# Attention block in one launch: the second normalised tensor's high part, the fourth inner cast and the last transposition change their places

## The chip, the cores and the metric

The kernel runs on one core of one Trainium2 chip. The core has TensorE for matrix products and transpositions (in the profile PE, its weight loads PEld), VectorE (DVE), ScalarE (ACT) and GpSimd (POOL) for elementwise work, and SyncE (SP), which here does nothing but start DMAs. The metric is the device time of one execution in microseconds. The kernel before takes 1758.4 us, the median of three runs from 1757.55 to 1760.98.

## The reference

The inputs are x and memory of 128 sequences by 128 rows by 256 features, a mask, and the weights of one block with 16 heads of 16 features:

```
tgt1 = layer_norm(x, g1, be1)
q, k, v = tgt1 @ Wq.T + bq, tgt1 @ Wk.T + bk, tgt1 @ Wv.T + bv
p = softmax(q k.T / 4 + (1 - mask) * -1e9)         # 16 heads
t = x + (p v) @ Wo.T + bo + (memory @ Wg.T + bg)
z = layer_norm(t, g2, be2)
out = t + relu(z @ W1.T + b1) @ W2.T + b2           # 256 -> 1024 -> 256
```

All of it is in fp32. The large products are made of three passes each: both operands are split into a high part (the value rounded to the type fp32r) and a low part (the rest), and a product is high by low, low by high, high by high. So each operand of a product costs a copy (the high part) and a subtraction (the low part), on whatever engine they are placed.

## The kernel before, in words

The 128 sequences are worked off in 64 groups of two. A loop over `i` from -2 to 65 is written out in full, and each pass works on several groups at once, one stage each: `norm` (first layer norm of group i+2), `front` (q, k and v of group i+1), `attn_` (scores, exponentials, transpositions of group i), `out_` (values, output product and second layer norm of group i-1) and `ffn` (the inner layer of group i-2). Each engine has its own copy of the loop, and within a pass 13 ticks `t`; what an engine does in what order is written out by hand as `if stage and t == n`, in program order. Engines wait for each other by semaphores alone, and an engine that waits holds up all that stands behind it on its queue. A pass takes some 26.4 us.

The second layer norm runs like this. TensorE makes the output product (ticks 5 and 6). VectorE adds the residual and takes the statistics (tick 7), GpSimd makes the inverse root (`rstd`, L867 and L869), VectorE makes the normalised tensor `xhat` in two instructions, one for each sequence (tick 8, `layer_norm_apply`, L617), and turns it in blocks of 32 by 32 into the buffer `attn` (`turn_quads`, L626). Four DMAs from SP bring the blocks back into `xhat` with the features on the partitions (L392). ScalarE then makes z's high part (`zT_hi`, `split_high`, L441, tick 12), VectorE its low part (`zT_lo`, L733, tick 0 of the next pass), and TensorE starts the first of four inner products with it (`up`, tick 1). ScalarE applies the relu to each of the four (ticks 3, 4, 5 and 7, L501), VectorE makes the high part (`hidden_high`, a CAST, L684), GpSimd the low part (`split_low`, L874), and TensorE contracts each of the four pairs back (`DOWN_TICKS`, 9 to 12).

On ScalarE the `zT_hi` of tick 12 stands ahead of `copy_inverses` (L468, the transposed inverse sums), and both ahead of the next pass's `copy_turned` of the last chunk (L460) and the first chunk's exponentials (L448). Later in that pass come `q_hi` (L488), further exponentials, the first relu (L501) and `k_hi` (L515), for which VectorE's `k_lo` (L788) waits. On VectorE the fourth `hidden_high` stands behind `xhat` and its transposition (L811 and L812), ahead of `v_pad`, `mask_bias` and the reciprocals. On GpSimd the fourth `hT_lo` stands behind `rstd` and ahead of `xT_hi` and `xT_lo` (L918, L923), the split of the first layer norm's tensor for the group behind.

Of the kernel before, what the change touches and what calls it, by code (L numbers as in the profile page):

```python
# [58 lines left out]
def is_at(i, n):  # L59

    return isinstance(i, int) and i == n
# [7 lines left out]
def xattn_block(nc, x, memory, mask, wqT, wkT, wvT, woT, wgT, w1T, w2T,  # L69
# [26 lines left out]
    with ExitStack() as ctx:  # L96
# [70 lines left out]
        for name, n in VECTORS:  # L167
# [56 lines left out]
        proj_ready, xres_biased, resid_ready = sem("proj_ready"), sem("xres_biased"), sem("resid_ready")  # L224
        ln2_stats, ln2_mean, ln2_var, ln2_rstd, ln2_ready = (
            sem(f"ln2_{n}") for n in ("stats", "mean", "var", "rstd", "ready"))
        z_blocked, z_cols, z_hi, z_split = (sem(f"z_{n}") for n in ("blocked", "cols", "hi", "split"))

        hid_ready, hid_relu, hid_hi, hid_split = (sem(f"s_hid_{n}") for n in ("ready", "relu", "hi", "split"))
# [92 lines left out]
        def _(sp):  # L322
# [29 lines left out]
            def iteration(i, norm, front, attn_, out_, ffn):  # L352
                if front:

                    g = i + 1
                    if g < 2:
                        sp.wait_ge(zeros_set, 2 * g + 2)
                    else:
                        sp.wait_ge(scores_ready, CHUNKS * (g - 1))
                    sp.wait_ge(q_split, g + 1)  # L360
                    for j, high_low in enumerate((1, 0, 0)):
                        sp.dma_start(q_stack[g % 2][j:P:CPB].bitcast(F32),
                                     q[high_low][:].bitcast(F32)).then_inc(q_stacked, 16)
                    sp.wait_ge(k_split, g + 1)
                    for e in range(2):
                        for j, high_low in enumerate((0, 1, 0)):
                            to = HALF * e + j
                            sp.dma_start(k_stack[g % 2][to:HALF * (e + 1):CPB, :, e].bitcast(F32),
                                         kk[high_low][HALF * e:HALF * (e + 1)].bitcast(F32)
                                         ).then_inc(k_stacked, 16)  # L370
                    if known(i, 1, GROUPS):
                        sp.wait_ge(mem_split, i)
                        sp.dma_start(mem_in[:], mem_cols[i]).then_inc(mem_loaded, 16)
                if is_at(i, GROUPS - 1):

                    sp.wait_ge(mem_split, i)
                    sp.dma_start(mem_in[:], mem_cols[i]).then_inc(mem_loaded, 16)
                if norm and i + 2 > 0:

                    sp.wait_ge(x_blocked, i + 2)  # L380
                    for n in range(QUADS):
                        sp.dma_start(x_flat[:, n * P:(n + 1) * P],
                                     x_blocks[32 * n:32 * (n + 1), :].rearrange("c (j n) -> c j n", j=QUADS)
                                     ).then_inc(x_cols, 16)
                if known(i, 1, GROUPS):
                    sp.wait_ge(resid_ready, i)
                    sp.dma_start(x_res[:], x_rows[i]).then_inc(xres_loaded, 16)
                if out_:

                    sp.wait_ge(z_blocked, i)  # L390
                    for n in range(QUADS):
                        sp.dma_start(xhat2_flat[:, n * P:(n + 1) * P],  # L392
                                     attn_blocks[32 * n:32 * (n + 1), :].rearrange("c (j n) -> c j n", j=QUADS)
                                     ).then_inc(z_cols, 16)
                if known(i, -1, GROUPS - 2):
                    sp.wait_ge(bias_ready, i + 2)
                    sp.dma_start(mask_in[:], mask_rows[i + 2]).then_inc(mask_loaded, 16)
                if known(i, -2, GROUPS - 3):
                    if i == -2:
                        sp.wait_ge(ln1_ready, 1)  # L400
                    elif i == -1:
                        sp.wait_ge(x_split, 2)
                    else:
                        sp.wait_ge(x_pool_split, i + 1)
                    sp.dma_start(x_in[:], x_rows[i + 3]).then_inc(x_loaded, 16)
                if attn_:

                    sp.wait_ge(inv_copied, i + 1)
                    if later(i):
                        sp.wait_ge(attn_ready, i)  # L410
                    heads = P // SPREADS
                    for b in range(GB):
                        for k in range(KT):
                            at = heads * (KT * b + k)
                            sp.dma_start(inv[:, k, b * S:(b + 1) * S],
                                         inv_cols[at:at + heads, :].unsqueeze(1)
                                         .broadcast_to([heads, P // heads, S])).then_inc(inv_spread, 16)
                if ffn:

                    sp.wait_ge(y_summed, i - 1)  # L420
                    sp.dma_start(out_rows[i - 2], y[:]).then_inc(y_stored, 16)
# [5 lines left out]
        def _(act):  # L427
# [42 lines left out]
            def iteration(i, norm, front, attn_, out_, ffn):  # L470
                for t in range(TICKS):
                    if out_ and t == 0:
                        copy_turned(i - 1, CHUNKS - 1)
                    if is_at(i, -1) and t == 0:
                        split_high(by_tile[1], xT[0][:], x_turned, 1, v_ready, None, x_hi)
                    if attn_ and t == EXP_TICKS[0]:
# [40 lines left out]
                        last.then_inc(k_high, 1)  # L517
                    if attn_ and t in (4, 6, 7, 9):
                        exponentials(i, CPB + (4, 6, 7, 9).index(t))
                    if out_ and t == 12:  # L520
                        g = i - 1
                        split_high(quad_cols(xhat2), in_order(zT[0]), z_cols, 16 * QUADS * (g + 1), hid_ready,
                                   HJ * g if later(g) else None, z_hi)
                    if attn_ and t == 12:
                        copy_inverses(i)

# [16 lines left out]
        def _(dve):  # L543
# [147 lines left out]
            def iteration(i, norm, front, attn_, out_, ffn):  # L691
                for t in range(TICKS):
# [18 lines left out]
                    if attn_ and t < CHUNKS:  # L711
# [15 lines left out]
                                in1=mask_bias[:, b, :], scale=1.0, scalar=HIGHEST, op0=ALU.add,  # L727
                                op1=ALU.min, accum_out=row_min[:, t, h:h + 1])
                        last.then_inc(scores_masked, 1)
                    if ffn and t == 0:  # L730
                        g = i - 2
                        dve.wait_ge(z_hi, g + 1)
                        dve.tensor_tensor(in_order(zT[1]), quad_cols(xhat2), in_order(zT[0]), ALU.subtract  # L733
                                          ).then_inc(z_split, 1)
# [37 lines left out]
                        dve.tensor_copy(attnT[0][:], attn[:]).then_inc(attnT_hi, 1)  # L772
                    if out_ and t == 4:
                        split_low(attn[:], attnT, attnT_hi, i, attnT_split)
                    if ffn and t in HIDDEN_TICKS and t < 8:
                        hidden_high(i - 2, HIDDEN_TICKS.index(t))
                    if norm and t == 4 and i != -1:
                        dve.wait_ge(x_loaded, 16 * (i + 3))
# [25 lines left out]
                    if out_ and t == 8:  # L804
                        g = i - 1
                        if later(g):
                            dve.wait_ge(z_split, g)
                        layer_norm_apply(g, resid, mv2, rstd2, ln2_rstd, xhat2, ln2_ready)
                        dve.wait_ge(attnT_split, g + 1)
                        turn_quads(attn_blocks, xhat2, ln2_ready, g + 1, z_blocked)  # L810
                    if ffn and t == HIDDEN_TICKS[-1]:  # L811
                        hidden_high(i - 2, HJ - 1)  # L812
                    if front and t == 9:
                        set_values(i + 1, 0)
                        set_values(i + 1, 1)
# [20 lines left out]
        def _(pool):  # L836
# [39 lines left out]
            def iteration(i, norm, front, attn_, out_, ffn):  # L876
                for t in range(TICKS):
                    if norm and t == 5:
                        inverse_root(i + 2, mv1, var1, rstd1, ln1_mean, ln1_var, ln1_ready, ln1_rstd)
                    if ffn and t in HIDDEN_TICKS:  # L880
                        g, n = i - 2, HIDDEN_TICKS.index(t)
                        if n == 0 and later(g):
                            pool.wait_ge(down_ready, g)
                        split_low(hid[:, n % 2], [h[:, 2 * n:2 * n + 2, :] for h in hT], hid_hi,
                                  HJ * g + n + 1, hid_split)
                    if out_ and t == 2:
                        g = i - 1
                        pool.wait_ge(mem_loaded, 16 * (g + 1))
# [40 lines left out]
        def _(pe):  # L929
# [122 lines left out]
            def iteration(i, norm, front, attn_, out_, ffn):  # L1052
                fronts, outs = stages_before(i)
                for t in range(TICKS):
# [60 lines left out]
                        last.then_inc(v_ready, 1)  # L1115
                    if ffn and t in UP_TICKS:
                        up(i, t)
                    if ffn and t in DOWN_TICKS:

                        g, part = i - 2, DOWN_TICKS.index(t)  # L1120
                        if part == 0 and i < GROUPS:
                            pe.wait_ge(hid_relu, HJ * g + HJ)
                        elif part == 0:
                            pe.wait_ge(y_summed, g)
                        pe.wait_ge(hid_split, HJ * g + part + 1)
                        for f in range(2 * part, 2 * part + 2):
                            for b in range(GB):
                                last = product(ffn_ps[:, b * D:(b + 1) * D],
                                               [(cut(hT, ALL, f, seq(b)), cut(w2, ALL, f))],
                                               start=(f == 0 and b == 0), stop=(f == FT - 1),  # L1130
                                               skip_group_check=True)
                        if part == HJ - 1:
                            last.then_inc(down_ready, 1)
# [44 lines left out]
```

## Time and profile before

| what | value |
|---|---|
| median of the runs | 1758.4 us |
| the profiled execution | 1759.22 us |
| its span, first to last instruction | 1757.3 us |
| PE busy | 1684.2 us, 96% |
| PEld busy | 1643.0 us, 93% |
| DVE busy | 1509.3 us, 86% |
| ACT busy | 1393.1 us, 79% |
| POOL busy | 953.5 us, 54% |
| granted TensorE clock, mean | 0.99 of full speed |

The busy shares are means over the whole span. The profile's 40 slices show the same pattern from the third to the last but one: the 64 groups are worked off in passes that are almost alike. What sets the length of a pass is read from the timeline of one pass; the passes between about 849 and 876 us are used below. In a timeline row the first number is the start in microseconds from the span's start, the second the time the row takes (for xN all of them), and the brackets say how long the engine was idle before and for whom it waited.

### The profile page before, as it was taken

Reading aid. Unit: us, or ns where it says so; the run is one execution under the profiler, and the core shown is the slowest. Engines: PE = TensorE matmul, PEld = TensorE weight load, DVE = VectorE, ACT = ScalarE, POOL = GpSimd, SP = SyncE. Lnnn points to the kernel's source line nnn. Section 1 sums busy time; section 2 is a strip of 40 time slices with the busy share of each in tenths; the row PEclk is TensorE's granted clock in tenths of the full one; section 3 lists DMA queues with packets and bytes.
Section 4 is the critical chain, followed back from the end, with each engine's and each line's share of the span. In section 5 each row is a group of like instructions: output and inputs, shape, how many; then the busy total and the mean of one; then the engine's idle time right before and its main releaser. Section 6 shows DMA issues by size and latency. Waiting matters only on the chain. (4 is left out here: it accounts for less than half of the span.)

```text
span 1757.3 us, 53486 instructions
## 1 busy us (share of the span) xinstructions
PE 1684.2 (96%) x17272; PEld 1643.0 (93%) x17272; DVE 1509.3 (86%) x7136; ACT 1393.1 (79%) x5506; POOL 953.5 (54%) x906
## 2 busy tenths in 40 slices
PE   6799999999999999999999999999999999999997
PEld 5699999999999999999999999999999999999997
DVE  7798898898888888888888888888888888888873
ACT  4788788788788788788788788788788787787782
POOL 5355545545545545555555555555555555555544
PEclk8899999999999999999999999999999999999999
DMA  5434444444444444444444444444444444444421
GB/s 187 130 124 138 140 131 138 131 139 132 134 142 130 137 140 130 136 141 131 136 145 128 136 142 131 135 142 132 134 139 136 133 141 135 128 146 135 128 91 37
DMA packets 258951, 233.77 MB, mean 133 GB/s; under 512 B 26992, under 2 KB 209136, under 8 KB 258672
## 3 DMA queue, kind: packets, MB, share of 16 engines
q1 hardware_dynamic: 258672, 230.35, 41.5%
q8 instruction: 139, 2.28, 0.6%
q14 instruction: 140, 1.15, 0.2%
HBM read 62.73 MB, written 16.78 MB: 45 GB/s over the span
## 5 line engine op out<-in xcount | busy, mean ns | idle before, releaser
L448 ACT ACTIVATE scores<-scores,row_min 128x128 f32<-128x128 f32 x2048 | 799.5, 406 | 37.1 <-DVE row_min L725 37.1
L874 POOL TENSOR_TENSOR hT_lo<-hid,hT_hi 128x512 fp32r<-128x512 f32 x256 | 339.6, 1327 | 687.7 <-DVE hT_hi L684 687.7
L725 DVE CUSTOM_DVE_ANT_0 scores<-score_ps,mask_bias 128x128 f32<-128x128 f32 x2048 | 467.8, 286 | 1.5 <-issue 1.1
L448 ACT ACTIVATION_READ_ACCUMULATOR scores<-scores,row_min 128x1 f32 x2048 | 420.5, 205 | 0.0
L460 ACT ACTIVATE probs<-turn_ps 128x512 f32<-128x512 f32 x512 | 306.3, 599 | 92.6 <-PE turn_ps L1022 92.6
L956 PE MATMUL ffn_ps<-w_hi,hT_lo 128*128 128x256 f32 x1024 | 301.2, 294 | 32.6 <-POOL hT_lo L874 32.2
L1022 PE MATMUL turn_ps<-ident,scores 128*128 128x128 f32 x2048 | 307.1, 273 | 5.3 <-ACT probs L460 5.3
L956 PE MATMUL ffn_ps<-zT_hi,w_lo 128*128 128x256 f32 x992 | 294.0, 296 | 1.4 <-ACT hid L501 1.2
L958 PE MATMUL ffn_ps<-w_hi,hT_hi 128*128 128x256 f32 x1024 | 284.2, 277 | 0.0
L957 PE MATMUL ffn_ps<-w_lo,hT_hi 128*128 128x256 f32 x1024 | 283.5, 277 | 0.0
L957 PE MATMUL ffn_ps<-zT_lo,w_hi 128*128 128x256 f32 x992 | 276.1, 278 | 0.0
L958 PE MATMUL ffn_ps<-zT_hi,w_hi 128*128 128x256 f32 x992 | 275.5, 278 | 0.0
L501 ACT ACTIVATE hid<-ffn_ps,vec 128x256 f32<-128x256 f32 x496 | 208.6, 481 | 43.9 <-PE ffn_ps L958 43.8
L1022 PEld LDWEIGHTS turn_ps<-ident,scores 128*128 128x128 f32 x2048 | 235.2, 140 | 6.1 <-ACT scores L448 6.1
L956 PEld LDWEIGHTS ffn_ps<-w_hi,hT_lo 128*128 128x128 f32 x1024 | 192.4, 188 | 47.3 <-POOL hT_lo L874 46.6
L1008 PE MATMUL score_ps<-k_stack,q_stack 128*128 128x256 f32 x1024 | 206.7, 294 | 2.3 <-DVE row_min L725 2.3
L956 PEld LDWEIGHTS ffn_ps<-zT_hi,w_lo 128*128 128x128 f32 x992 | 187.2, 189 | 14.6 <-issue 12.3
L957 PEld LDWEIGHTS ffn_ps<-w_lo,hT_hi 128*128 128x128 f32 x1024 | 193.0, 189 | 0.0
L958 PEld LDWEIGHTS ffn_ps<-w_hi,hT_hi 128*128 128x128 f32 x1024 | 192.3, 188 | 0.0
L957 PEld LDWEIGHTS ffn_ps<-zT_lo,w_hi 128*128 128x128 f32 x992 | 187.0, 188 | 0.0
L958 PEld LDWEIGHTS ffn_ps<-zT_hi,w_hi 128*128 128x128 f32 x992 | 186.3, 188 | 0.0
L725 DVE DVE_READ_ACCUMULATOR2_ANT row_min<- 128x1 f32 x2048 | 168.9, 82 | 0.0
(144 smaller groups left out, 4288.0 us busy)
## 6 DMA issues: line engine op xcount, KB each, us to landing
q_stack<-q_hi SPq DMA_DIRECT2D x128, 256.0 KB, 2.4
k_stack<-k_hi SPq DMA_DIRECT2D x256, 128.0 KB, 2.3
x_in<-x_dram SPq DMA_DIRECT2D x64, 256.0 KB, 2.7
mem_in<-memory_dram SPq DMA_DIRECT2D x64, 256.0 KB, 3.0
x_res<-x_dram SPq DMA_DIRECT2D x64, 256.0 KB, 3.0
q_stack<-q_lo SPq DMA_DIRECT2D x64, 256.0 KB, 2.3
k_stack<-k_lo SPq DMA_DIRECT2D x128, 128.0 KB, 2.3
inv<-inv_cols SPq DMA_DIRECT2D x256, 64.0 KB, 2.4
```

What stands on the lines that cost most here:

```text
L448: last = act.activation(exps, exps, ACT.Exp, bias=row_min[:, k, h:h + 1], scale=-1.0, accum_out=row_sum[:, k, h:h + 1])
L460: act.activation(probs[:, k, :], turn_ps[k % 2][:, :], ACT.Copy).then_inc(probs_copied[k % 2], 1)
L501: last = act.activation(hid[:, n % 2, j, :], up_bank(i, n)[:, j * ROWS:(j + 1) * ROWS], ACT.Relu, bias=b1c[:, 2 * n + j:2 * n + j + 1])
L725: last = dve.tensor_tensor_reduce(out=scores[:, slot(i, t), h, :], in0=score_ps[t % 2][:, h * S:(h + 1) * S], in1=mask_bias[:, b, :], scal ...
L874: pool.tensor_tensor(halves[1], src, halves[0], ALU.subtract).then_inc(done, 1)
L956: pe.matmul(dst, lhs[1], rhs[0], start=start and j == 0, stop=False, **more)
L957: pe.matmul(dst, lhs[0], rhs[1], start=False, stop=False, **more)
L958: last = pe.matmul(dst, lhs[0], rhs[0], start=False, stop=stop and j == n - 1, **more)
L1008: last = pe.matmul(score_ps[n % 2][:, k * 2 * S:(k + 1) * 2 * S], q_stack[i % 2][:, c, k, seq(b)], k_stack[i % 2][:, c, :, GB * k + b, :], ...
L1022: last = pe.transpose(turn_ps[k % 2][:, h * S:(h + 1) * S], scores[:, slot(g, k), h, :], ident[:])
```

## The change

Four things are edited, and a semaphore `z_turned` is added.

1. On ScalarE, `zT_hi` leaves tick 12 and stands at tick 0 of the next pass, behind `copy_turned` of the last chunk and ahead of the first exponentials. `copy_inverses` and that `copy_turned` so come ahead of it.
2. On VectorE, `zT_lo` goes from tick 0 to tick 1, behind the masking of the second chunk's scores.
3. On VectorE, all four `hidden_high` are now issued in the same place of their ticks, so the fourth (tick 8) comes ahead of `xhat` and its transposition.
4. For the last group alone, `xhat` isn't turned in blocks and moved by the four DMAs. TensorE transposes it with four products by the identity into the bank `work[1]` (before the last contraction of pass 64), and ScalarE and VectorE take high and low part from there.

```diff
@@ SP, iteration
-                if out_:
+                if out_ and i < GROUPS:
 
                     sp.wait_ge(z_blocked, i)
@@ ScalarE, iteration
                     if out_ and t == 0:
                         copy_turned(i - 1, CHUNKS - 1)
+                    if is_at(i, GROUPS + 1) and t == 0:
+                        split_high(by_tile[1], zT[0][:], z_turned, 1, hid_ready, HJ * (GROUPS - 1), z_hi)
+                    elif ffn and t == 0:
+                        g = i - 2
+                        split_high(quad_cols(xhat2), in_order(zT[0]), z_cols, 16 * QUADS * (g + 1), hid_ready,
+                                   HJ * g if later(g) else None, z_hi)
...
-                    if out_ and t == 12:
-                        g = i - 1
-                        split_high(quad_cols(xhat2), in_order(zT[0]), z_cols, 16 * QUADS * (g + 1), hid_ready,
-                                   HJ * g if later(g) else None, z_hi)
                     if attn_ and t == 12:
                         copy_inverses(i)
@@ VectorE, iteration
-                    if ffn and t == 0:
+                    if is_at(i, GROUPS + 1) and t == 1:
+                        split_low(by_tile[1], zT, z_hi, GROUPS, z_split)
+                    elif ffn and t == 1:
                         g = i - 2
                         dve.wait_ge(z_hi, g + 1)
...
-                    if ffn and t in HIDDEN_TICKS and t < 8:
+                    if ffn and t in HIDDEN_TICKS:
                         hidden_high(i - 2, HIDDEN_TICKS.index(t))
...
                         layer_norm_apply(g, resid, mv2, rstd2, ln2_rstd, xhat2, ln2_ready)
-                        dve.wait_ge(attnT_split, g + 1)
-                        turn_quads(attn_blocks, xhat2, ln2_ready, g + 1, z_blocked)
-                    if ffn and t == HIDDEN_TICKS[-1]:
-                        hidden_high(i - 2, HJ - 1)
+                        if i < GROUPS:
+                            dve.wait_ge(attnT_split, g + 1)
+                            turn_quads(attn_blocks, xhat2, ln2_ready, g + 1, z_blocked)
@@ TensorE, iteration
+                    if is_at(i, GROUPS) and t == 12:
+                        pe.wait_ge(ln2_ready, GROUPS)
+                        pe.wait_ge(resid_ready, GROUPS)
+                        turn(by_tile[1], xhat2).then_inc(z_turned, 1)
                     if ffn and t in DOWN_TICKS:
```

VectorE's queue from the second layer norm's statistics to the addition that ends the inner layer, in a pass of the middle, before the change (the dots leave out the masking of one chunk's scores):

```order
L611 BN_AGGR mv<-stats 128x2 x2
...
L617 SCALAR_TENSOR_TENSOR xhat<-resid,mv,rstd 128x256 x2
L626 STREAM_TRANSPOSE attn<-xhat 128x2x4x32 x2
L684 CAST hT_hi<-hid 128x512
L666 TENSOR_TENSOR v_pad<-work_ps,row 128x8x16 x4
L821 TENSOR_SCALAR mask_bias<-mask_in 128x256
```

The same place of the same queue with the change:

```order
L614 BN_AGGR mv<-stats 128x2 x2
...
L687 CAST hT_hi<-hid 128x512
L620 SCALAR_TENSOR_TENSOR xhat<-resid,mv,rstd 128x256 x2
L629 STREAM_TRANSPOSE attn<-xhat 128x2x4x32 x2
L669 TENSOR_TENSOR v_pad<-work_ps,row 128x8x16 x4
L825 TENSOR_SCALAR mask_bias<-mask_in 128x256
```

The cast of the fourth inner pair has moved ahead of the two `xhat` instructions and the two transpositions; all else keeps its order.

ScalarE's queue across the boundary of two passes, before the change (`probs` are the turned chunks, `inv_cols` the inverse sums):

```order
L460 ACTIVATE probs<-turn_ps 128x512
L441 ACTIVATE zT_hi<-xhat 128x512
L468 ACTIVATE inv_cols<-turn_ps 128x128
L460 ACTIVATE probs<-turn_ps 128x512
L448 ACTIVATE scores,row_sum<-scores,row_min 128x128 x4
L488 ACTIVATE q_hi<-work_ps,qk_bias 128x256 x2
```

And with the change:

```order
L461 ACTIVATE probs<-turn_ps 128x512
L469 ACTIVATE inv_cols<-turn_ps 128x128
L461 ACTIVATE probs<-turn_ps 128x512
L442 ACTIVATE zT_hi<-xhat 128x512
L449 ACTIVATE scores,row_sum<-scores,row_min 128x128 x4
L495 ACTIVATE q_hi<-work_ps,qk_bias 128x256 x2
```

`zT_hi` has moved behind the inverse sums and the last turned chunk; it still stands ahead of the exponentials. GpSimd's queue is unchanged in order.

## Rows read from the trace of the kernel before

**Rows 1.** View of waits, whole span: who waited for whom, us, times, longest.

```profile
ACT zT_hi L441 <- DMA xhat<-attn: 148.6, 64, 7.0
...
PEld ffn_ps L956 <- POOL hT_lo L874: 46.6, 61, 1.4
...
PE ffn_ps L956 <- POOL hT_lo L874: 32.2, 61, 1.2
```

**Rows 2.** Timeline of TensorE at the fourth contraction of one pass.

```profile
871.81 0.60 PE L1022 MATMUL turn_ps<-ident,scores 128*128 128x128 f32 x4
872.90 0.38 PE L956 MATMUL ffn_ps<-w_hi,hT_lo 128*128 128x256 f32 x1 [0.49 <-POOL hT_lo L874]
```

**Rows 3.** Timeline of VectorE in the same pass.

```profile
859.41 0.84 DVE L788 SCALAR_TENSOR_TENSOR k_lo<-work_ps,qk_bias,k_hi 128x256 fp32r<-128x256 f32 x2
...
861.02 0.42 DVE L684 CAST hT_hi<-hid 128x512 fp32r<-128x512 f32 x1
861.36 1.92 DVE L617 SCALAR_TENSOR_TENSOR x_in<-x_in,mv,rstd 128x256 f32<-128x256 f32 x2
863.38 1.18 DVE L626 STREAM_TRANSPOSE x_quads<-x_in 128x256 f32<-128x256 f32 x2
...
868.48 0.28 DVE L725 CUSTOM_DVE_ANT_0 scores<-score_ps,mask_bias 128x128 f32<-128x128 f32 x1
869.03 0.88 DVE L617 SCALAR_TENSOR_TENSOR xhat<-resid,mv,rstd 128x256 f32<-128x256 f32 x2 [0.26 <-POOL rstd L869]
```

**Rows 4.** Timeline of GpSimd in the same pass.

```profile
861.52 1.47 POOL L874 TENSOR_TENSOR hT_lo<-hid,hT_hi 128x512 fp32r<-128x512 f32 x1 [0.67 <-DVE hT_hi L684]
...
868.24 0.69 POOL L869 TENSOR_TENSOR rstd<-var,minus_half 128x2 f32<-128x2 f32 x1
871.58 1.27 POOL L874 TENSOR_TENSOR hT_lo<-hid,hT_hi 128x512 fp32r<-128x512 f32 x1 [2.65 <-DVE hT_hi L684]
872.80 1.10 POOL L918 TENSOR_TENSOR xT_hi<-x_in,one 128x512 fp32r<-128x512 f32 x1
```

**Rows 5.** Timeline of ScalarE from one zT_hi to the next.

```profile
848.89 0.63 ACT L441 ACTIVATE zT_hi<-xhat 128x512 fp32r<-128x512 f32 x1 [2.21 <-DMA xhat<-attn]
849.43 0.26 ACT L468 ACTIVATE inv_cols<-turn_ps 128x128 f32<-128x128 f32 x1
...
850.07 0.40 ACT L448 ACTIVATE scores<-scores,row_min 128x128 f32<-128x128 f32 x1
...
855.40 0.84 ACT L501 ACTIVATE hid<-ffn_ps,vec 128x256 f32<-128x256 f32 x2
...
858.13 0.85 ACT L515 ACTIVATE k_hi<-work_ps,qk_bias 128x256 fp32r<-128x256 f32 x2
...
875.23 0.63 ACT L441 ACTIVATE zT_hi<-xhat 128x512 fp32r<-128x512 f32 x1 [2.18 <-DMA xhat<-attn]
```

**Rows 6.** Timeline of TensorE at the second inner product of that pass.

```profile
856.37 0.37 PE L956 MATMUL ffn_ps<-zT_hi,w_lo 128*128 128x256 f32 x1
```

**Rows 7.** Timelines of VectorE and GpSimd in the set-up.

```profile
21.80 1.00 POOL L869 TENSOR_TENSOR rstd<-var,minus_half 128x2 f32<-128x2 f32 x1
22.34 0.43 DVE L591 CAST wv_hi<-scores 128x512 fp32r<-128x512 f32 x1
26.28 4.98 POOL L856 TENSOR_TENSOR w_lo<-probs,w_hi 128x2048 fp32r<-128x2048 f32 x1
26.98 1.20 DVE L626 STREAM_TRANSPOSE x_quads<-x_in 128x256 f32<-128x256 f32 x2
```

**Rows 8.** The chain that ended last, its tail: start us, us, what.

```profile
1736.94 2.14 DMA xhat<-attn
...
1741.12 0.38 PE score_ps L956
```

**Rows 9.** View of stretches: busy us by engine, then the granted TensorE clock (1.00 is full).

```profile
1738.40:1741.10 2.70, 0.00 (x0) 0.00 (x0) 1.99 (x2) 0.63 (x1) 1.26 (x1) 1.00 0.34 114
1742.20:1745.60 3.40, 3.40 (x18) 3.40 (x18) 0.43 (x1) 0.84 (x2) 0.90 (x1) 0.51 0.00 0
```

More of the change, by code:

```diff
@@ L226, in xattn_block @@
             sem(f"ln2_{n}") for n in ("stats", "mean", "var", "rstd", "ready"))
+        z_turned = sem("z_turned")
         z_blocked, z_cols, z_hi, z_split = (sem(f"z_{n}") for n in ("blocked", "cols", "hi", "split"))
@@ L883, in iteration @@
                             pool.wait_ge(down_ready, g)
-                        split_low(hid[:, n % 2], [h[:, 2 * n:2 * n + 2, :] for h in hT], hid_hi,
-                                  HJ * g + n + 1, hid_split)
+                        split_low(hid[:, n % 2], [h[:, 2 * n:2 * n + 2, :] for h in hT],
+                                  hid_hi, HJ * g + n + 1, hid_split)
                     if out_ and t == 2:
```

## The prediction

> **What bounds the kernel now.** I read the page first, then the view of waits, then the timeline of one pass for each engine. The page shows TensorE busy nearly throughout, and 61 almost equal passes: the question is what sets the length of one. The view of waits [rows 1] gives TensorE one wait that comes in every pass: the low part of the inner layer from GpSimd, 46.6 us at its weight loads in 61 waits, 0.76 us each (32.2 us by the matmul rows, which count the end of the product before as busy; I take the larger, since TensorE starts its next product 1.09 us after the transposition of a chunk [rows 2] and nothing but the wait explains so long a step). The other wait of that size is ScalarE's for the DMAs of `xhat`, 148.6 us in 64, which holds TensorE up nowhere so far.
>
> The timeline says where the 0.76 us come from. The fourth cast of `hid` stands behind `xhat` and its transposition on VectorE, so GpSimd's subtraction runs from 871.58 to 872.85 [rows 4] and the fourth contraction begins at 872.90 [rows 2]. TensorE could have begun it at about 872.1.
>
> A pass is 26.34 us by the two `zT_hi` [rows 5]; over the 61 passes it is 26.4.
>
> **The change part by part.**
>
> The cast that moves ahead (edit 3). The masking of the eighth chunk ends at about 868.7 and `xhat` starts at 869.03 behind an idle time of 0.26 us for `rstd` [rows 3]. The cast takes the next instruction's place for 0.34 us (861.02 to 861.36, the same pair of rows [rows 3]), so it fits this idle time and `xhat` can still start at 869.03. GpSimd's subtraction starts 0.08 us after a cast ends (861.44 to 861.52 [rows 3, 4]), here at about 869.15 instead of 871.58, and is done near 870.5, where TensorE wants it at 872.1. The wait is gone: 0.76 us in each of 61 passes, 46.6 us. That is the whole gain if nothing else gives way.
>
> What gives way is `xhat`. The two instructions of `xhat` take 0.88 us, with GpSimd silent. The same operation on `x_in`, with the same shapes, takes 1.92 us [rows 3]: it stands directly behind the second cast, and GpSimd's subtraction starts 0.16 us after it and takes 1.47 us instead of 1.27 [rows 4]. So the two engines keep each other off: one half runs, then GpSimd's whole subtraction, then the other half. The change makes exactly this picture at `xhat`: cast, two such instructions, and a GpSimd subtraction that starts some 0.1 to 0.15 us after the first. The price is 1.92 - 0.88 = 1.04 us. From below it would be 0 (GpSimd as if silent), from above GpSimd's time before the first half and another GpSimd operation between the halves (a rival). I take 1.04, since it is the row nearest in every respect. The block transposition behind it pays nothing: in the set-up it took 1.20 us for its two in the middle of a GpSimd subtraction of 4.98 us, as 1.18 beside an idle GpSimd [rows 3, 7].
>
> [...]
>
> What hangs on `xhat`. It is followed by the transposition, the four DMAs and `zT_hi`: from the start of `xhat` to the start of `zT_hi` 875.23 - 869.03 = 6.20 us [rows 3, 5], now 7.24. Edit 1 takes the inverse sums and the chunk's copy out from behind `zT_hi`: from `zT_hi` to the exponentials it was 850.07 - 848.89 = 1.18 us and is now `zT_hi`'s own step, 849.43 - 848.89 = 0.54 [rows 5]. So ScalarE begins the exponentials 1.04 - 0.64 = 0.40 us later than before, where TensorE wants to be 0.76 earlier. It works without a gap from there: exponentials, `q_hi`, two more chunks, the first relu. That relu ends at 856.24 and TensorE's second inner product begins at 856.37 [rows 5, 6], with 0.13 us to spare. There TensorE will wait about 0.7 us; the wait has moved.
>
> Whether this is a loop of its own decides the length of a pass, so I close it. From the exponentials ScalarE needs 858.98 - 850.07 = 8.91 us to the end of `k_hi` [rows 5]; `k_lo` on VectorE waits for it (0.05 us for the hand-over); from `k_lo` VectorE works without a gap to `xhat`, 869.03 - 859.41 = 9.62 [rows 3]; then 6.20 to the next `zT_hi` and 0.54 to the exponentials. The sum is 8.91 + 0.05 + 9.62 + 6.20 + 0.54 = 25.32 us without the stall and 26.36 with it. TensorE alone would do with 26.34 - 0.76 = 25.58. The loop now is as long as the old pass of 26.34 to 26.40: the gain of 46.6 us is given back, but for 0 to 2 us; I take 1.
>
> In this loop DMAs that land late are paid in full, which ScalarE's idle time hid before. The wait for them is (148.6 - 7.0) / 63 = 2.25 us in the mean and 2.18 to 2.21 in the rows of a quiet pass [rows 1, 5]: 63 x 0.05 = 3 us if all is paid, 0 if none. I take 2.
>
> `zT_lo` one chunk later (edit 2). VectorE's second masking takes about 0.85 us and fills the time in which `zT_hi` isn't there. If GpSimd's next operation holds the subtraction up, it ends at about 878.3, and TensorE's first inner product starts at about 879: 0.6 us of cover, so nothing. If that cover were gone, it would cost what is missing, once a pass.
>
> GpSimd's `xT_hi` follows the fourth subtraction (872.80 [rows 4]) and comes 1.3 to 2.3 us earlier; nobody waited for it. SP's four DMAs keep their place; those behind them (mask, `x_in`, inverse rows) aren't held up by anything new.
>
> The last group (edit 4). Before, from the end of `xhat` to the first product: the transposition, the DMAs (the last of them 1736.94 to 1739.08), 0.6 us for the high part, 1.3 for the low part, product at 1741.12 [rows 8]. Now TensorE transposes behind its third contraction (about 0.5 us), and high and low part overlap the fourth contraction, the addition of `y` and 0.7 us of subtraction. I get the first product at about 1738.5, 2.6 us earlier. [...] So the tail gives 2.6 to 4.3 us; I take 4, with some tenths from `copy_inverses` coming earlier in pass 63.
>
> **The sum**, on the profiled execution: 1759.2 (span 1757.3 and 1.9 around it) - 1 + 2 - 4 = 1756.2. This execution is 0.8 above the median of the runs, so 1755.4 us.
>
> **The rivals.**
>
> *The stall stays out.* If `xhat` gets through beside GpSimd, the loop is 25.32 and TensorE binds with 25.58: ScalarE starts the exponentials 0.64 us earlier against TensorE's 0.76, and 0.13 of spare time covers the difference. Then 1759.2 - 46.6 + 2 - 4 - 0.8 = 1710 us. For it: the cause is read from another place. Against: the row of `x_in` has the same neighbours, and 61 such passes show it. Partial forms, a stall that eats half of the gain, lie near 1733. Together 0.22.
>
> *GpSimd gets in first.* The cast falls into GpSimd's `rstd` (868.24 to 868.93 [rows 4]). In the set-up an `rstd` with a VectorE cast over its end took 1.00 us instead of 0.69 and ended at 22.80, just behind the cast (22.77) [rows 7]. If that happens here, `rstd` ends near 869.08 and `xhat` starts near 869.18, with GpSimd's subtraction already begun. Then both halves wait for its end near 870.42: 0.15 + 1.24 + 0.88 instead of 1.92, 0.35 us more a pass, 61 x 0.35 = 21 us: 1776 us. If `xT_hi`, which is then ready, also goes between the halves (1.10 us [rows 4]), it is 1.45 us a pass, 88 us: 1844. The point from which it decides is the order of two starts, GpSimd's subtraction and the first `xhat`, which I see within 0.05 us of each other in this case. Against it: one row of the set-up carries it, and there other VectorE work also lay beside `rstd`. 0.14 for the mild form, 0.08 for the full one.
>
> **How the numbers follow.** My forecast, the wait that moves from GpSimd's subtraction to the relu, has 0.50 and by its own bounds lies between 1749 and 1762. The other two have 0.22 and 0.22, and 0.06 is left for what I don't see, evenly to both sides. What a measurement of this kernel can tell from no change is 0.2%, 3.5 us, so the line to faster is at 1754.9, in the middle of my forecast: 0.23 of its 0.50 is faster, 0.25 the same, 0.02 slower. With the rivals: faster 0.23 + 0.22 + 0.03 = 0.48, slower 0.02 + 0.22 + 0.03 = 0.27, the same 0.25. The range from 1706 to 1778 takes in the forecast, the first rival and the mild form of the second, 0.86, and leaves out its full form.
>
> **What would show it.** TensorE's wait for `hT_lo` falls from 46.6 us to a few. `xhat` takes 1.92 us for its two (0.88 refutes me towards 1710), starting before GpSimd's subtraction; if the subtraction comes first, the second rival holds. TensorE or its weight loads get a wait of 30 to 45 us in all for the relu of ScalarE (L508) at the second inner product, and `k_lo` follows `k_hi` at once. ScalarE's wait for the DMAs shrinks to some 0.3 to 0.8 us a pass, since it now does the inverse sums and a chunk's copy while they are under way. The passes stay at 26.3 to 26.4 us; at 25.6 my loop is wrong. In the tail the first product of the last group comes about 2.6 us earlier against the end of the third contraction, and the granted clock stays at 1.00 behind it or not.

## The result and the profile after

The kernel became slower, well past what the forecast allowed: 1818.07 us with the change (median of four runs, 1815.37 to 1820.07) against 1759.68 before (1757.55 to 1760.98), a ratio of 1.0332 with a 95% interval of 1.0312 to 1.0352. The profiled execution took 1819.23 us with a span of 1817.5, 60.2 more than before. The mean granted clock is 0.992 of full, so the time isn't lost there.

The page with the change (busy time, share of the span, instructions of each engine):

```profile
PE 1698.5 (93%) x17276; PEld 1642.2 (90%) x17276; DVE 1618.5 (89%) x7134; ACT 1407.5 (77%) x5506; POOL 976.6 (54%) x906
```

The view of waits with the change (us in total, times, longest), which answers to [rows 1]:

```profile
PEld turn_ps L1034 <- DVE sum_inv L655: 55.5, 62, 5.2
...
ACT zT_hi L442 <- DMA xhat<-attn: 48.4, 60, 2.2
DVE zT_lo L738 <- ACT zT_hi L442: 47.5, 62, 2.2
PEld ffn_ps L960 <- ACT hid L508: 47.2, 62, 1.6
...
PEld ffn_ps L960 <- DVE zT_lo L738: 28.7, 59, 1.7
DVE k_lo L793 <- ACT k_hi L522: 20.6, 56, 1.3
```

TensorE's wait for `hT_lo` is gone, as meant. In its place come three: for the relu of ScalarE at the second inner product (the one forecast), for the reciprocals and for `zT_lo`. `k_lo` now waits for `k_hi` in 56 passes. ScalarE is late once a pass, and the waits for the relu, for `zT_lo` and for `k_hi` are downstream of it. The reciprocals stand behind `xhat` and its transposition on VectorE's queue and come late with them.

VectorE in a pass of the middle (start us, us, operation, idle time before), which answers to [rows 3]:

```profile
890.70 0.88 DVE L793 SCALAR_TENSOR_TENSOR k_lo<-work_ps,qk_bias,k_hi 128x256 fp32r<-128x256 f32 x2 [0.96 <-ACT k_hi L522]
...
892.34 0.43 DVE L687 CAST hT_hi<-hid 128x512 fp32r<-128x512 f32 x1
892.68 1.92 DVE L620 SCALAR_TENSOR_TENSOR x_in<-x_in,mv,rstd 128x256 f32<-128x256 f32 x2
...
900.00 0.42 DVE L687 CAST hT_hi<-hid 128x512 fp32r<-128x512 f32 x1
900.57 2.69 DVE L620 SCALAR_TENSOR_TENSOR xhat<-resid,mv,rstd 128x256 f32<-128x256 f32 x2
903.37 1.19 DVE L629 STREAM_TRANSPOSE attn<-xhat 128x256 f32<-128x256 f32 x2
```

GpSimd at the same place, which answers to [rows 4]:

```profile
899.55 0.91 POOL L873 TENSOR_TENSOR rstd<-var,minus_half 128x2 f32<-128x2 f32 x1
900.51 1.29 POOL L878 TENSOR_TENSOR hT_lo<-hid,hT_hi 128x512 fp32r<-128x512 f32 x1
901.76 1.22 POOL L922 TENSOR_TENSOR xT_hi<-x_in,one 128x512 fp32r<-128x512 f32 x1
```

This is the answer in two views. `rstd` takes 0.91 us instead of 0.69 and ends at 900.46, 0.04 behind the cast's end (900.42). GpSimd's subtraction follows it at 900.51, VectorE's first half of `xhat` at 900.57: GpSimd is first by 0.06 us. The pair now takes 2.69 us where it took 0.88, and its end (903.26) lies 0.28 behind the end of `xT_hi` (902.98), the second GpSimd operation. By these ends, both GpSimd operations have gone ahead of the second half. In 54 of the 57 passes of the middle it is so.

ScalarE, from the high part of `z` on, in the same pass and the next, which answers to [rows 5]:

```profile
881.76 0.39 ACT L449 ACTIVATE scores<-scores,row_min 128x128 f32<-128x128 f32 x1
...
887.10 0.82 ACT L508 ACTIVATE hid<-ffn_ps,vec 128x256 f32<-128x256 f32 x2
...
889.83 0.83 ACT L522 ACTIVATE k_hi<-work_ps,qk_bias 128x256 fp32r<-128x256 f32 x2
...
908.62 0.63 ACT L442 ACTIVATE zT_hi<-xhat 128x512 fp32r<-128x512 f32 x1 [0.67 <-DMA xhat<-attn]
909.16 0.39 ACT L449 ACTIVATE scores<-scores,row_min 128x128 f32<-128x128 f32 x1
```

TensorE in this stretch, which answers to [rows 2, 6]:

```profile
887.97 0.39 PE L960 MATMUL ffn_ps<-zT_hi,w_lo 128*128 128x256 f32 x1 [1.39 <-ACT hid L508]
...
903.49 0.60 PE L1026 MATMUL turn_ps<-ident,scores 128*128 128x128 f32 x4
903.85 0.37 PE L960 MATMUL ffn_ps<-w_hi,hT_lo 128*128 128x256 f32 x1
```

The fourth contraction begins 0.36 us after the transposition of a chunk (before: 1.09), and the second inner product 0.05 us after the relu's end (887.92) with 1.39 us of idle time. The wait has moved, and grown.

The loop of the prediction closes with these rows: 8.90 (exponentials at 881.76 to the end of `k_hi` at 890.66) + 0.04 + 9.87 (`k_lo` to `xhat`) + 2.80 (`xhat` to its transposition) + 5.25 (to `zT_hi`) + 0.54 = 27.40 us. The passes from `zT_hi` to `zT_hi` have a median of 27.40 and a mean of 27.50 (before: 26.40 and 26.46). A loop over ScalarE, VectorE and the DMAs sets the pass, and TensorE waits for it.

The tail, on VectorE, which answers to [rows 8]:

```profile
1797.06 1.82 DVE L620 SCALAR_TENSOR_TENSOR xhat<-resid,mv,rstd 128x256 f32<-128x256 f32 x2 [0.29 <-POOL rstd L873]
...
1802.13 0.68 DVE L692 TENSOR_TENSOR zT_lo<-work_ps,zT_hi 128x512 fp32r<-128x512 f32 x1
```

TensorE in the tail:

```profile
1799.51 0.60 PE L977 MATMUL work_ps<-ident,xhat 128*128 128x128 f32 x4
...
1802.86 0.38 PE L960 MATMUL score_ps<-zT_hi,w_lo 128*128 128x256 f32 x1 [1.38 <-DVE zT_lo L692]
```

The view of stretches for the time behind it, with the granted clock as the third number from the end, which answers to [rows 9]:

```profile
1802.80:1806.20 3.40, 3.34 (x29) 3.34 (x30) 0.43 (x2) 1.15 (x3) 1.05 (x2) 1.00 0.22 77
```

From the start of the last `xhat` to the first product of the last group it is 5.80 us (before 8.23), and from there to the last `y` 11.4 (before 13.03). TensorE stood idle for 1.38 us instead of 2.7 and ran on at a granted clock of 1.00 (29 matmuls in 3.34 us) instead of 0.51 (18 in 3.40 us). The tail gave 4.0 us.

### The profile page after: what moved, and what is told of

Read it like the earlier page. It is cut to its first block and busy times, and to the rows that moved or that the text cites. A ratio compares the mean times of both kernels' runs of the same rounds, so it can differ in the third digit from the quotient of the medians.

```text
span 1817.5 us, 53488 instructions
## 1 busy us (share of the span) xinstructions
PE 1698.5 (93%) x17276; PEld 1642.2 (90%) x17276; DVE 1618.5 (89%) x7134; ACT 1407.5 (77%) x5506; POOL 976.6 (54%) x906
## 5 line engine op out<-in xcount | busy, mean ns | idle before, releaser
L449 ACT ACTIVATION_READ_ACCUMULATOR scores<-scores,row_min 128x1 f32 x2048 | 410.0, 200 | 0.0
L620 DVE SCALAR_TENSOR_TENSOR xhat<-resid,mv,rstd 128x256 f32<-128x256 f32 x128 | 165.5, 1331 | 8.8 <-POOL rstd L873 0.5
```

The costliest lines, as they stand in the source:

```text
L449: last = act.activation(exps, exps, ACT.Exp, bias=row_min[:, k, h:h + 1], scale=-1.0, accum_out=row_sum[:, k, h:h + 1])
L620: last = dve.scalar_tensor_tensor(out=dst[:, b, :], in0=src[:, b, :], scalar=mv[:, b, 0:1], in1=rstd[:, b:b + 1].broadcast_to([P, D]), op0 ...
```

## The experiments

The theory: the cast moved ahead of `xhat` (edit 3) costs all of it. It lies over the end of `rstd`, which ends later; GpSimd then starts its subtraction ahead of `xhat` and its `xT_hi` ahead of the second half. The rivals: the move of `zT_hi` (edits 1 and 2) makes ScalarE and TensorE late; or the time is GpSimd's subtraction as such, whenever it lies beside `xhat`.

All figures of a pass are medians over 56 or 57 passes of the middle. "Step" is from the first `xhat` to its transposition; "GpSimd" is the start of its fourth subtraction against that of `xhat`; the loop is summed as above, with 1.17 + 4.07 us from the transposition to `zT_hi`, and 0.54 or (without edit 1) 1.17 us from there to the exponentials. Each ratio is against runs of the kernel before that were taken beside that version, so the first row has a span of medians.

| kernel | time, us | ratio, interval | pass | `rstd` | `k_lo` to `xhat` | step | GpSimd | loop |
|---|---|---|---|---|---|---|---|---|
| before | 1758.3 to 1759.7 | | 26.40 | 0.69 | 9.63 | 0.99 | +2.5 | 25.96 |
| changed | 1818.07 | 1.0332, 1.0312 to 1.0352 | 27.40 | 0.91 | 9.88 | 2.79 | -0.06 | 27.39 |
| cast alone | 1868.0 | 1.0624, 1.0607 to 1.0640 | 28.04 | 0.91 | 9.88 | 2.80 | -0.06 | 28.02 |
| without the cast | 1754.46 | 0.9972, 0.9962 to 0.9982 | 26.39 | 0.69 | 9.63 | 0.99 | +2.5 | 25.33 |
| last z alone | 1754.93 | 0.9978, 0.9969 to 0.9987 | 26.39 | 0.69 | 9.63 | 0.99 | +2.5 | 25.96 |
| `xT_hi` waits | 1777.89 | 1.0112, 1.0096 to 1.0128 | 26.61 | 0.91 | 9.88 | 2.01 | -0.06 | 26.60 |
| cast waits for `rstd` | 1783.57 | 1.0137, 1.0118 to 1.0157 | 26.79 | 0.69 | 10.00 | 2.02 | +0.16 | 26.73 |
| low part waits | 1724.87 | 0.9810, 0.9796 to 0.9824 | 25.78 | 0.91 | 9.85 | 0.99 | +0.96 | 25.55 |
| cast between | 1721.38 | 0.9794, 0.9772 to 0.9816 | 25.77 | 0.69 | 9.63 | 1.14 | +1.30 | 25.48 |
| cast between, on before | 1746.9 | 0.9942, 0.9922 to 0.9962 | 26.15 | 0.69 | 9.66 | 1.13 | +1.3 | 26.13 |

### Edit 3 alone, on the kernel before

```diff
-                    if ffn and t in HIDDEN_TICKS and t < 8:
+                    if ffn and t in HIDDEN_TICKS:
                         hidden_high(i - 2, HIDDEN_TICKS.index(t))
...
-                    if ffn and t == HIDDEN_TICKS[-1]:
-                        hidden_high(i - 2, HJ - 1)
```

> The kernel before with edit 3 alone (the fourth cast ahead of xhat); z's high part stays in tick 12, ahead of the inverse sums. Theory L (loop): a pass is as long as the loop exponentials - k_hi - k_lo - xhat - DMAs - zT_hi, and xhat is held up by GpSimd (2.05 us with the later start). With the old ScalarE order the way from zT_hi to the exponentials is 1.18 instead of 0.54, so 27.40 + 0.64 = 28.04 us a pass and about 1760 + 61 x 1.64 = 1860 us. Rival Z: z's parts are late because edits 1 and 2 put them later, and the cast is innocent: then this kernel is no slower than before, 1715 to 1760 us.

It took 1868.0 us, 6.2% more than before and 50 us more than the whole change. VectorE, and then ScalarE over one pass:

```profile
891.17 2.69 DVE L617 SCALAR_TENSOR_TENSOR xhat<-resid,mv,rstd 128x256 f32<-128x256 f32 x2
```

```profile
871.18 0.63 ACT L441 ACTIVATE zT_hi<-xhat 128x512 fp32r<-128x512 f32 x1 [3.94 <-DMA xhat<-attn]
...
899.22 0.63 ACT L441 ACTIVATE zT_hi<-xhat 128x512 fp32r<-128x512 f32 x1 [3.93 <-DMA xhat<-attn]
```

The pair takes the same 2.69 us, and the pass is 28.04. So edit 3 alone has the whole damage, and edit 1 takes 0.64 us a pass off it: just the inverse sums and the copy that it moves from behind `zT_hi`.

### Edits 1, 2 and 4 without edit 3

The diff is the one above, undone on the changed kernel.

> The changed kernel without edit 3 (the fourth cast back behind xhat and its transposition); edits 1, 2 and 4 stay. Theory L: xhat's pair takes 0.88 us again, TensorE waits for GpSimd's fourth low part again (about 46 us), a pass is 26.4 us, and with the shorter tail the time is about 1755 us. Rival Z: the pass stays near 27.4 us and the time near 1818.

It took 1754.46 us. The loop would allow 25.33, but the pass stays at 26.39, since TensorE waits for GpSimd's low part as before:

```profile
PEld ffn_ps L962 <- POOL hT_lo L880: 38.0, 60, 1.0
```

The move of `zT_hi` costs nothing and by itself gives nothing; the first rival falls. What this version gains is the tail.

### The last z alone (edit 4), on the kernel before

```diff
-                if out_:
+                if out_ and i < GROUPS:
                     sp.wait_ge(z_blocked, i)
...
```

With it come the branches of the last pass on ScalarE, VectorE and TensorE, as in the change.

> The kernel before with edit 4 alone: the last group's xhat is transposed by TensorE instead of blocks and DMAs. The kernel with edits 1, 2 and 4 took 1754.5 against 1758.7. If the tail is all of that, this one takes about 1755 us too, and the passes stay at 26.40. If the other ScalarE and VectorE order gave the gain, it takes about 1758.

It took 1754.93 us, 3.4 us less than the kernel before beside it (1758.34), with the passes unchanged. The tail was forecast with 4.

### GpSimd's second operation held back

```diff
@@ GpSimd, ahead of xT_hi
+                        if out_ and i < GROUPS:
+                            pool.wait_ge(z_blocked, i)
```

> The changed kernel, but GpSimd's xT_hi waits until xhat is transposed; the fourth subtraction still starts ahead of xhat. Theory L with two parts of the stall: GpSimd's subtraction ahead of the first half (stays) and xT_hi between the halves (gone). The step from xhat to the transposition falls from 2.79 us to the 2.01 that the last passes without an xT_hi show, rstd stays at 0.91, a pass is 27.40 - 0.78 = 26.62 us and the time about 1818 - 47 = 1771 us. If xT_hi is not in it, the step stays at 2.79 and the time at 1818.

VectorE, then GpSimd:

```profile
877.96 1.91 DVE L620 SCALAR_TENSOR_TENSOR xhat<-resid,mv,rstd 128x256 f32<-128x256 f32 x2
879.97 1.17 DVE L629 STREAM_TRANSPOSE attn<-xhat 128x256 f32<-128x256 f32 x2
```

```profile
877.89 1.29 POOL L878 TENSOR_TENSOR hT_lo<-hid,hT_hi 128x512 fp32r<-128x512 f32 x1
881.31 1.04 POOL L924 TENSOR_TENSOR xT_hi<-x_in,one 128x512 fp32r<-128x512 f32 x1 [2.13 <-DVE attn L629]
```

GpSimd is still first by 0.06 us (877.89 to 877.96), but only its subtraction holds `xhat` up: 1.91 us. The pass falls by 0.79 us to 26.61, as expected (26.62). So `xT_hi` between the halves is 0.78 of the 1.80 us by which the step grew. The time of 1777.89 is 7 us over the expectation of 1771.

### The forecast's picture restored: the cast waits for rstd

```diff
@@ VectorE, hidden_high
+                if n == HJ - 1 and g + 1 < GROUPS:
+                    dve.wait_ge(ln2_rstd, g + 2)
```

> The changed kernel, but VectorE's fourth cast waits until rstd is done; it still stands ahead of xhat, and GpSimd isn't held back. This makes the picture that the prediction forecast: rstd 0.69 us, the first xhat half ahead of GpSimd's subtraction, a step of 2.02 us from xhat to the transposition. Theory L: the cast then costs its own 0.34 us behind rstd (k_lo to xhat 9.63 + 0.34 = 9.97), the loop is 8.90 + 0.03 + 9.97 + 2.02 + 1.17 + 4.07 + 0.54 = 26.70 us, and the time about 1818 - 61 x 0.70 = 1775 us. If the order of the two starts made no difference, the step would stay at 2.79 us and the time near 1823.

VectorE, then GpSimd:

```profile
885.85 0.43 DVE L689 CAST hT_hi<-hid 128x512 fp32r<-128x512 f32 x1 [0.26 <-POOL rstd L875]
886.20 1.91 DVE L620 SCALAR_TENSOR_TENSOR xhat<-resid,mv,rstd 128x256 f32<-128x256 f32 x2
```

```profile
885.06 0.69 POOL L875 TENSOR_TENSOR rstd<-var,minus_half 128x2 f32<-128x2 f32 x1
886.36 1.47 POOL L880 TENSOR_TENSOR hT_lo<-hid,hT_hi 128x512 fp32r<-128x512 f32 x1 [0.61 <-DVE hT_hi L689]
```

With the cast behind `rstd`, `rstd` takes 0.69 us again, the subtraction starts 0.16 us after `xhat`, and the step is 2.02 us: the picture and the price of `x_in` in [rows 3]. The cast costs its own 0.37 us, since it now stands in the way of `xhat` (10.00 to `xhat` instead of 9.63). The forecast's loop of 26.36 and these 0.37 make 26.73; measured were 26.79. The time was 1783.57 against an expected 1775.

### The low part held back behind xhat

```diff
@@ GpSimd, ahead of split_low
+                        if n == HJ - 1 and out_:
+                            pool.wait_ge(ln2_ready, i)
```

> The changed kernel, but GpSimd's fourth subtraction waits until both xhat instructions are done; the cast stays ahead of xhat. Theory L with the cause in the GpSimd subtraction: the pair takes 0.88 us, rstd still 0.91 because the cast lies over its end, so the loop is 25.32 + 0.25 = 25.57 us, TensorE alone 25.6, about 1711 us. If instead the cast itself or its place on VectorE is what slows xhat, the pair stays at 2.69 us and the time at 1818.

VectorE, then GpSimd:

```profile
880.38 0.42 DVE L687 CAST hT_hi<-hid 128x512 fp32r<-128x512 f32 x1
880.94 0.88 DVE L620 SCALAR_TENSOR_TENSOR xhat<-resid,mv,rstd 128x256 f32<-128x256 f32 x2
```

```profile
879.93 0.91 POOL L873 TENSOR_TENSOR rstd<-var,minus_half 128x2 f32<-128x2 f32 x1
881.91 1.29 POOL L878 TENSOR_TENSOR hT_lo<-hid,hT_hi 128x512 fp32r<-128x512 f32 x1 [1.07 <-DVE xhat L620]
```

The cast keeps its place, and `rstd` is stretched as before, but the pair is back at 0.88 us and the kernel at 1724.87, 1.9% under the one before. This separates the two prices of edit 3: 0.22 to 0.25 us for `rstd`, which doesn't bind here, and 1.80 for the step. The time missed its expectation (1711) by 14 us.

### The cast between xhat and its transposition

```diff
                         layer_norm_apply(g, resid, mv2, rstd2, ln2_rstd, xhat2, ln2_ready)
+                    if ffn and t == HIDDEN_TICKS[-1]:
+                        hidden_high(i - 2, HJ - 1)
+                    if out_ and t == 8:
                         if i < GROUPS:
...
```

(and the condition at the other ticks is `t < 8` again.)

> The changed kernel with the fourth cast between the two xhat instructions and the block transposition. Theory L: GpSimd's subtraction starts after xhat is made, rstd takes 0.69 us again, the pair 0.88; the transposition comes 0.34 us later and nothing holds it up. The loop is 25.32 + 0.34 = 25.66 us, TensorE alone 25.6: about 1760 - 61 x 0.74 - 4 = 1711 us. Rival R: after the wait for the low part TensorE is held by the reciprocals of the inverse sums (55 us of waiting in the changed kernel) whatever xhat does; then the pass stays above 26.3 us and the time above 1750.

VectorE, then GpSimd, then the wait that TensorE is left with:

```profile
878.35 0.88 DVE L620 SCALAR_TENSOR_TENSOR xhat<-resid,mv,rstd 128x256 f32<-128x256 f32 x2 [0.27 <-POOL rstd L876]
879.15 0.42 DVE L687 CAST hT_hi<-hid 128x512 fp32r<-128x512 f32 x1
879.48 1.16 DVE L629 STREAM_TRANSPOSE attn<-xhat 128x256 f32<-128x256 f32 x2
```

```profile
877.55 0.69 POOL L876 TENSOR_TENSOR rstd<-var,minus_half 128x2 f32<-128x2 f32 x1
879.65 1.30 POOL L881 TENSOR_TENSOR hT_lo<-hid,hT_hi 128x512 fp32r<-128x512 f32 x1 [1.40 <-DVE hT_hi L687]
```

```profile
PEld ffn_ps L963 <- ACT hid L508: 9.8, 18, 1.3
```

GpSimd's subtraction now lies beside the transposition, which takes 1.16 us as without it. Nothing is stretched. This version has the lowest median, 1721.38 us: 2.1% under the kernel before (by the interval 1.8 to 2.3%) and 5.3% under the changed one. The low part held back, 3.5 us above it, is not clearly apart from it, since the two intervals overlap. It was expected at 1711, with a pass of 25.66; the pass is 25.77, though its loop needs only 25.48. The low part held back gives 25.78 with a loop of 25.55. Two different loops with one pass: here TensorE's own work is the bound, and it is longer than my 25.58. In most passes TensorE has no wait left for the relu (9.8 us in 18). The removed wait was worth 26.40 - 25.77 = 0.63 us a pass, between the 0.49 of the matmul row [rows 2] and the 0.76 of the weight loads. These versions rule out the second rival too: the subtraction costs by its place, not as such. The rival named in the expectation falls as well: TensorE's wait for the reciprocals goes from 55.5 us in 62 to 6.9 us in 2.

### The same on the kernel before (without edits 1, 2 and 4)

> The kernel before with the fourth cast between xhat and its transposition, and nothing else. Theory L: with the old ScalarE order (1.18 us from zT_hi to the exponentials) the loop is 8.90 + 0.03 + 9.63 + 1.14 + 1.17 + 4.07 + 1.17 = 26.11 us, longer than TensorE's own 25.77, so a pass is 26.1 us and the time about 1760 - 61 x 0.29 = 1742 us; edits 1 and 2 are worth some 17 us once the cast stands here. If TensorE alone bounds it, 25.77 us a pass and about 1725 us.

It took 1746.9 us with a pass of 26.15, where the loop gives 26.13 (expected 26.11 and 1742):

```profile
PEld ffn_ps L957 <- ACT hid L501: 25.6, 62, 1.3
```

With `zT_hi` in its old place the loop binds before TensorE does. So edits 1 and 2 together are worth 0.38 us a pass (26.15 - 25.77) once the cast is out of the way, and 0 while TensorE waits for GpSimd; no run separates the two.

## Why the prediction was wrong

Forecast were 1755.4 us (1706 to 1778); it took 1818.07, outside the range. What happened was the case to which I gave 0.08.

**The step that failed** is the first price of edit 3: "it fits this idle time and `xhat` can still start at 869.03", with GpSimd's subtraction "some 0.1 to 0.15 us after the first". The cast does fit VectorE's idle time, but it isn't free for GpSimd: `rstd`, under way on the other engine, ends 0.22 us later. Then both engines are released by the same moment, the end of `rstd`: in the pass shown GpSimd goes on 0.05 us after it and VectorE 0.11, so GpSimd is first by 0.06. Had `rstd` ended 0.22 us earlier, `xhat` would have come directly behind the cast, at 900.34, and the subtraction only at 900.50; this is an estimate from these rows and the 0.34 and 0.08 us that the prediction read. That this lies in the lateness of `rstd` is shown from both sides: where the cast lies over the end of `rstd` (changed, cast alone, `xT_hi` waits, low part waits) it takes 0.91; where it doesn't (cast between, without the cast, cast waits for `rstd`) 0.69. The changed kernel shows it within itself, too. In three of the 57 passes VectorE lost a little time inside the masking ahead of the cast, so the cast started 0.62 to 0.80 us after `rstd` instead of 0.45. GpSimd in one of them, and VectorE:

```profile
762.41 0.69 POOL L873 TENSOR_TENSOR rstd<-var,minus_half 128x2 f32<-128x2 f32 x1
763.63 1.47 POOL L878 TENSOR_TENSOR hT_lo<-hid,hT_hi 128x512 fp32r<-128x512 f32 x1 [0.52 <-DVE hT_hi L687]
765.05 1.23 POOL L922 TENSOR_TENSOR xT_hi<-x_in,one 128x512 fp32r<-128x512 f32 x1
```

```profile
762.49 0.29 DVE L728 CUSTOM_DVE_ANT_0 scores<-score_ps,mask_bias 128x128 f32<-128x128 f32 x1 [0.17 <-issue]
...
763.12 0.42 DVE L687 CAST hT_hi<-hid 128x512 fp32r<-128x512 f32 x1
763.46 1.92 DVE L620 SCALAR_TENSOR_TENSOR xhat<-resid,mv,rstd 128x256 f32<-128x256 f32 x2
765.48 1.17 DVE L629 STREAM_TRANSPOSE attn<-xhat 128x256 f32<-128x256 f32 x2
```

`rstd` is through at 763.10, 0.02 us before the cast starts. `xhat` gets in 0.17 us ahead of the subtraction, the pair takes the 1.92 us of the forecast, and `xT_hi` no longer comes between the halves. A small delay of VectorE made the step shorter.

Of the 1.02 us by which the pass exceeds the forecast's loop (27.38 against 26.36), 0.25 is the late `rstd` and 0.77 is `xT_hi` between the halves. The order of the two starts costs nothing by itself: with GpSimd first but `xT_hi` held back the step is 2.01 us, with VectorE first 2.02. What GpSimd's lead does is to let a second GpSimd operation in ahead of the second half.

The prediction had the evidence: the row of the set-up with 1.00 instead of 0.69 [rows 7], and the remark that the order of two starts decides, "within 0.05 us of each other". It gave 0.22 to all of this because other VectorE work lay beside that one row. The nearest row was the right one, though, and what stood against it was only a doubt.

**The other steps.**

- The picture behind the stall held. At `xhat`, the measured order of starts decides who is held up: +0.16 us costs 1.03 (2.02 - 0.99) and makes GpSimd's subtraction 1.47 us instead of 1.29, -0.06 us costs 1.02 without a second GpSimd operation and 1.80 with it. At `rstd` the order of starts doesn't tell it: `rstd` had started some 0.45 us ahead of the cast, and yet it ended 0.22 us late, 0.04 us behind the cast, in each of the 54 passes. I had counted on the two engines holding each other up at `xhat`, and at `rstd` only in a rival.
- The loop was right in kind and in sum. With the measured terms it gives the pass of the five kernels in which it binds within 0.06 us, and lies under the pass in the other five, where TensorE binds: in three of them with its wait for GpSimd's low part, in two with its own work. With the forecast's it was 26.36; the pass grew by 0.25 (to `xhat`) and 0.77 (the step, 2.79 instead of 2.02), which makes 27.38.
- The full form was over-priced: 1.45 us a pass above the forecast's loop, measured 1.04. I had put the two GpSimd operations ahead of the whole pair, but the halves overlap them: the second ends only 0.28 us after `xT_hi`.
- The wait for the relu came (47.2 us in 62, forecast 30 to 45), `k_lo` follows `k_hi` at once, and ScalarE's wait for the DMAs fell to 0.8 us a pass (forecast 0.3 to 0.8).
- The late DMAs were under-sized: 2 us forecast. From the end of the transposition to `zT_hi` the median is 4.07 us before and after, but the mean rose from 4.10 to 4.21 and is now paid whole. That is (4.21 - 4.07) x 57 = 8 us: in 6 of the 57 passes the set lands 0.6 to 1.6 us late, in others by a tenth or two. The other kernels in which the loop binds have means of 4.2 to 4.3. This, with TensorE's own 25.77, is most of the 5 to 14 us by which six of the eight versions above missed their expectations.
- Edit 2 was put at nothing, with 0.6 us of cover for `zT_lo`. TensorE does wait for it in the changed kernel, 28.7 us in 59, but only 3.8 us in 5 with the cast between: the wait follows from ScalarE's lateness and is no term of its own. The largest of TensorE's new waits, 55.5 us for the reciprocals, wasn't foreseen; it isn't on the loop either.
- TensorE alone: 25.58 forecast, 25.77 measured. It bears only on the rival of 1710, which would have come to about 1722, as the two best versions show.
- The tail: -4 forecast, -4.0 by its rows, -3.4 by the run of edit 4 alone. Over the 2.6 us of the earlier first product the 4 has a term (up to 1.7 us) that no run shows. What the runs showed in its place: the first product came 2.43 us earlier (5.80 against 8.23), the granted clock stayed at 1.00 behind 1.38 us of idle time, and the way from there to the last `y` was 1.63 us shorter (11.40 against 13.03).

**The sum as measured**, against the span before: 1.04 x 57 = 59 us of pass for the passes of the middle by their means, -4 for the tail, and some 5 in the first and last passes, by difference; together 60.2. Of the 59, the late DMAs have some 8 and the moved cast the rest.

**What stays open**: why some of the four DMAs land late; no experiment took that up. And why both GpSimd operations get in ahead of the second half of `xhat`, where in the three odd passes the halves and the subtraction take turns; only the two patterns were measured.

## What to carry to other kernels

Before moving an operation into another engine's idle time, look at what the neighbours run in that same instant, and at which pair of instructions is released by the same event: a short cast over the end of a 128x2 operation made it 0.22 us late, and that turned the order of two starts and let a second GpSimd operation in. The step grew by 1.80 us where 1.04 had been forecast, in each of some 60 passes. Find the loop over the engines that closes on itself and keep its sum beside that of the bounding engine: a gain on the one is worth only the distance to the other. Where a row of the profile, however lone, shows the stretched case, place the moved operation where that case can't arise: two instructions later, the same cast made the kernel about 2% faster.

## What the runs showed that I had not expected

- The cast of 128x512 (0.42 us) took `rstd`, an operation on 128x2 elements, from 0.69 to 0.91 us, though it lay over no more than its end; in the pass shown they ended 0.04 us apart.
- 0.06 us of lead for GpSimd or 0.16 for VectorE is the difference between a step of 2.79 and one of 2.02 us, pass after pass, within 0.02 us, as long as a second GpSimd operation is ready.
- The block transposition isn't held up by a GpSimd subtraction beside it: 1.16 us with it (cast between) and 1.17 without.
